# A mixture-of-experts router: gate products with the token columns stationary, choice of experts on the logits

## What is computed

```python
raw_gate = softmax(einsum('btd,de->bte', x, gate), axis=-1)      # 4096 tokens, 256 -> 16 logits
_, topk_idx = lax.top_k(raw_gate, 3)
mask = one_hot(topk_idx, 16).sum(axis=2)
gate_topk = mask * raw_gate
gate_topk = gate_topk / maximum(sum(abs(gate_topk), axis=-1), 1e-12)
hidden = relu(einsum('btd,edh->bteh', x, W1) + b1)
expert_out = einsum('bteh,ehd->bted', hidden, W2) + b2
out = einsum('bte,bted->btd', gate_topk, expert_out)
```

## Time and profile before

| | us |
|---|---|
| median of 3 runs (1891.88 to 1895.51) | 1894.03 |
| the profiled execution, its own time | 1896.07 |
| span of the profiled execution | 1894.1 |
| PE busy in the span | 1727.0 (91%) |
| DVE busy | 1362.5 (72%) |
| POOL busy | 1263.0 (67%) |
| ACT busy | 743.8 (39%) |
| routing phase (first transposes to last decoding) | 1308.4 to 1407.5 |

### The profile page before, as it was taken

How to read it: one execution, slowest core, us unless ns; L and a number is a source line. 1 busy time by engine, 2 the same in 40 slices (tenths; PEclk the granted TensorE clock), 3 DMA queues, 4 the chain that set the end, 5 groups by cost and what they waited for, 6 DMA issues and landing times. The chain is left out here.

```text
span 1894.1 us, 33741 instructions
## 1 busy us (share of the span) xinstructions
PE 1727.0 (91%) x9587; PEld 1288.4 (68%) x9588; DVE 1362.5 (72%) x3170; ACT 743.8 (39%) x1583; POOL 1263.0 (67%) x1086
## 2 busy tenths in 40 slices
PE   5389999999999999999999999998679999999970
PEld 4356766766666676667667666754349999999960
DVE  3358888888888888888888888865974544444435
ACT  3124445444445544444444445534442222222213
POOL 2138778767887786787778688833347777777753
PEclk8579999999999999999999999999659999999995
DMA  9856656755665676556657646613944444444447
GB/s 308 283 167 172 174 148 187 211 146 156 187 166 153 197 201 177 168 153 191 180 181 213 164 144 169 177 47 118 374 137 69 71 72 74 73 71 73 72 83 234
DMA packets 184483, 300.41 MB, mean 159 GB/s; under 512 B 22544, under 2 KB 81936, under 8 KB 184352
## 3 DMA queue, kind: packets, MB, share of 16 engines
q1 hardware_dynamic: 160784, 267.23, 47.8%
q0 software_dynamic: 21504, 30.29, 9.9%
q10 hardware_dynamic: 2064, 1.31, 0.2%
HBM read 186.84 MB, written 111.67 MB: 158 GB/s over the span
## 5 line engine op out<-in xcount | busy, mean ns | idle before, releaser
L735 ACT ACTIVATE prob<-b_ps 128x512 f32<-128x512 f32 (+3 forms) x768 | 354.6, 488 | 364.3 <-PE b_ps L572 260.7
L499 POOL TENSOR_TENSOR acc<-acc,prob 128x1024 f32<-128x1024 f32 (+1 forms) x192 | 353.1, 1839 | 6.4 <-POOL acc L499 3.2
L571 PE MATMUL b_ps<-q,k 128*128 128x512 f32 (+3 forms) x768 | 296.9, 391 | 9.7 <-DMA q<-mrow 5.2
L472 POOL TENSOR_TENSOR roped<-rot 128x512 f32<-128x512 f32 x128 | 175.0, 1367 | 184.6 <-DVE rot L858 183.8
L564 PE MATMUL a_ps<-k,q 128*128 128x512 f32 (+3 forms) x768 | 267.5, 385 | 18.6 <-DMA k<-scratch_hilo 9.7
L840 DVE CUSTOM_DVE_ANT_0 masked<-a_ps,causal 128x128 bf16<-128x128 f32 (+3 forms) x512 | 237.3, 479 | 58.8 <-PE a_ps L564 50.9
L653 PE MATMUL y_ps<-prob,v_sb 128*64 128x512 f32 (+3 forms) x1536 | 275.6, 494 | 0.0
L1573 DVE TENSOR_SCALAR hT<-h_ps,b1T 128x128 f32<-128x128 f32 x448 | 126.1, 344 | 197.4 <-PE h_ps L1489 158.4
L572 PE MATMUL b_ps<-q,k 65*128 65x512 f32 (+3 forms) x768 | 265.1, 349 | 0.0
L1463 POOL DMA_INDIRECT scratch_sum<-y,dst_i x112 | 177.8, 1587 | 95.6 <-ACT y L1538 90.8
L888 DVE RECIPROCAL inv<-inv 128x128 f32<-128x128 f32 x256 | 232.3, 929 | 8.6 <-ACT inv L776 6.2
(11 more groups left out here) (258 smaller groups left out, 2478.4 us busy)
## 6 DMA issues: line engine op xcount, KB each, us to landing
q<-scratch_hilo SPq DMA_DIRECT2D x192, 256.0 KB, 4.6
k<-scratch_hilo SPq DMA_DIRECT2D x192, 256.0 KB, 5.2
scratch_hilo<-hi SPq DMA_DIRECT2D x64, 512.0 KB, 4.2
scratch_hilo<-lo SPq DMA_DIRECT2D x64, 512.0 KB, 4.6
w_sb<-scratch_wsplit SPq DMA_DIRECT2D x32, 512.0 KB, 3.7
w<-in_L_ffn_W_dram SPq DMA_DIRECT2D x32, 512.0 KB, 9.3
wv_sb<-scratch_wsplit SPq DMA_DIRECT2D x16, 512.0 KB, 6.5
xT<-scratch_xsplit SPq DMA_DIRECT2D x6, 1024.0 KB, 6.9
```

Of the source, the lines that this page charges most:

```text
L499: nc.gpsimd.tensor_tensor(sums, old, probs(q), ALU.add).then_inc(m["sum_p"], 1)
L571: nc.tensor.matmul(out, k1[s][:, h, js], q1[s][:, h, qs], start=True, stop=False, skip_group_check=True)
L735: nc.scalar.activation(probs(q)[:, h, :], b_ps[:, h, 0:w], ACT.Exp).then_inc(exp_done[h], 1)
```

## The change

`gate_logits` swaps the operands: the 128 columns of a tile are stationary and the gate's half (16 columns) moves, so the logits come out with tokens on partitions, directly in the group's bank. `take_logits` (ACT) and `turn_logits` (PE) are gone, with their buffers. `choose` works on the logits in PSUM: eight largest, difference to the first of them, indices, one-hot matrices, mask; it no longer waits for the exponentials. `weigh` waits for them, multiplies them by the mask and divides by the sum of what is left. The floor of 1e-12 is gone (the largest exponential is 1).

```diff
             def gate_logits(u):
                 pe.wait_ge(m["r_xtt"], u + 1)
-                if u >= 4 and u % 2 == 0:
-                    pe.wait_ge(m["r_lt"], u // 2 - 1)
+                if u >= 8 and u % 4 == 0:
+                    pe.wait_ge(m["r_sub"], u // 4 - 1)
                 x_cols = xtt[:, u % 2, :].rearrange("p (i k c) -> p i k c", i=2, k=DK)
-                for k in range(DK):
-                    ins = nc.tensor.matmul(lt_ps[u // 2 % 2][0:E_, (u % 2) * 256:(u % 2) * 256 + 256], gate[:, k, :],
-                                           x_cols[:, :, k, :], start=(k == 0), stop=(k == DK - 1),
-                                           skip_group_check=True)
+                for i in range(2):
+                    for k in range(DK):
+                        ins = nc.tensor.matmul(logits_of(u // 4)[:, 2 * (u % 4) + i, :], x_cols[:, i, k, :], gate[:, k, :],
+                                               start=(k == 0), stop=(k == DK - 1), skip_group_check=True)
                 ins.then_inc(m["r_lg"], 1)
-            def turn_logits(v):
...
-                if u >= 3 and u % 2 == 1:
-                    turn_logits(u // 2 - 1)
...
-            turn_logits(UNITS // 2 - 1)
...
-            def take_logits(v):
...
-                if u >= 2 and u % 2 == 0:
-                    take_logits(u // 2 - 1)
...
-            take_logits(TILES // 4 - 1)
             exponents(GROUPS - 1)
...
-                dve.wait_ge(m["r_lgt"], 2 * (g + 1))
-                lg, some, sums = logits_of(g), red[:, 0, ts], red[:, 1, ts]
-                link(V.tensor_reduce(some, lg, AX_X, ALU.max))
-                V.tensor_tensor(tmp[:, ts], lg, bc(some, E_), ALU.subtract).then_inc(m["r_sub"], 1)
-                dve.wait_ge(m["r_exp"], g + 1)
-                link(V.tensor_reduce(some, prob[:, ts], AX_X, ALU.add))
-                link(V.reciprocal(sums, some))
-                link(V.tensor_tensor(prob[:, ts], prob[:, ts], bc(sums, E_), ALU.mult))
-                for t in range(ts.start, ts.stop):
-                    ins = V.max(top[:, t, :], prob[:, t, :])
+                dve.wait_ge(m["r_lg"], 4 * (g + 1))
+                lg = logits_of(g)
+                for i, t in enumerate(range(ts.start, ts.stop)):
+                    ins = V.max(top[:, t, :], lg[:, i, :])
                 link(ins)
-                for t in range(ts.start, ts.stop):
-                    ins = V.max_index(topi[:, t, :], top[:, t, :], prob[:, t, :])
-                link(ins)
-                V.tensor_reduce(some, top[:, ts, 0:TOPK], AX_X, ALU.add)
+                V.tensor_tensor(tmp[:, ts], lg, top[:, ts, 0:1].broadcast_to([P, LG, E_]), ALU.subtract)
+                for i, t in enumerate(range(ts.start, ts.stop)):
+                    ins = V.max_index(topi[:, t, :], top[:, t, :], lg[:, i, :])
+                ins.then_inc(m["r_sub"], 1)
+                dve.wait_ge(m["r_sub"], g + 1)
...
-                link(V.tensor_scalar(some, some, 1e-12, None, ALU.max))
-                V.reciprocal(sums, some)
...
-            def weigh(ts):
-                n = ts.stop - ts.start
+            def weigh(g):
+                ts = tiles_of(g)
+                some, sums = red[:, 0, ts], red[:, 1, ts]
+                dve.wait_ge(m["r_mask"], g + 1)
+                dve.wait_ge(m["r_exp"], g + 1)
                 link(V.tensor_tensor(tmp[:, ts], prob[:, ts], maskb[:, ts], ALU.mult))
-                link(V.tensor_tensor(tmp[:, ts], tmp[:, ts], bc(red[:, 1, ts], E_), ALU.mult))
+                link(V.tensor_reduce(some, tmp[:, ts], AX_X, ALU.add))
+                link(V.reciprocal(sums, some))
+                link(V.tensor_tensor(tmp[:, ts], tmp[:, ts], bc(sums, E_), ALU.mult))
```

More of the change, by code:

```diff
@@ L989, in routing_phase @@
         all_ps = ctx.enter_context(nc.psum_tensor("all_ps", [P, 512], F32))
-        lt_ps = [all_ps, pre_ps]
-        lt_sb = [slots, inc]
         bb_ps = ctx.enter_context(nc.psum_tensor("bb_ps", [P, 512], F32))
@@ L1004, in routing_phase @@
         names = ("r_slots r_begun r_ef r_row r_tile r_part r_code r_bb_sb r_inv r_stored r_bb r_bbadd r_w r_small r_const r_chain "
-                 "r_x1 r_xtr r_xtt r_lg r_lt r_lgt r_b1 r_rs r_sub "
+                 "r_x1 r_xtr r_xtt r_lg r_b1 r_rs r_sub "
                  "r_exp r_mask r_pre r_g32 r_gtr r_gt r_b2 r_b2hi r_b2lo r_zero r_gst").split()
@@ L1328, in _ @@
                 if g < GROUPS - 1:
-                    dve.wait_ge(m["r_mask"], g + 1)
-                    weigh(tiles_of(g))
+                    weigh(g)
                 if g == 2:
@@ L1335, in gate_weights @@
             def gate_weights():
-                dve.wait_ge(m["r_mask"], GROUPS)
-                weigh(tiles_of(GROUPS - 1))
+                weigh(GROUPS - 1)
                 link(V.tensor_copy(g32[:, :, 0:E_], tmp[:]))
```

## The result

| | before | after |
|---|---|---|
| median of 12 runs | 1894.55 us | 1898.55 us (1896.40 to 1905.85) |
| ratio of the runs, 95% interval | | 1.0025 (1.0015 to 1.0035) |
| span of the profiled execution | 1894.1 us | 1900.6 us |
| first transposes of the routing phase to its last decoding | 99.2 us | 106.0 us |
| last mask, counted from the first transposes | 37.6 us | 44.2 us |

The change makes the kernel slower by 4 us. The forecast was faster by 7; the first rival came. What stands outside the routing phase did not change, but the start of the phase varies: the code of the attention phase is the same in all kernels here, and the first transposes behind it started between 1300.8 and 1312.2 us.

The account below looks back on a forecast made before the run. The prediction took PE as the bound until the first group's logits, then DVE for four groups. Last mask 7.1 us earlier, weights 0.3 us longer: -6.8 us, giving a median of 1887.2 us, range 1884 to 1903.5.

Parts of the forecast that it names:

- the first rival: PE's clock falls to 1.2 GHz in the routing units, making the kernel slower: 1904.5 us, chance 0.27.
- The likeliest case: The forecast with its faster neighbour: routing phase shortened by 6.8 us, median 1887.2 us, chance 0.57.
- Part 2: PE's units: PE's routing units: removed turns save 2.4 us, swapped products add 1.2 us, last products end at 1334.9.
- the clock falls in the units: PE drops to 1.2 GHz after four routing units, adding 17.3 us to the units: 1904.5 us, chance 0.27.
- The term "products": PE's swapped gate products in each unit: 1.05 us in place of 0.97.
- The spacing: Swapped product records on PE follow each other at 0.114 us, eight of them making 0.91 us.
- the first load: First stationary load of each unit's products on PE, taken as uncovered: 0.08 us more per unit.
- Part 1: DVE's choice: 3.87 us a group up to the mask, weights 1.22 us, reads of PSUM costing no more.
- Part 3: Where PE and DVE meet: PE delivers a group every 6.6 us, DVE needs 5.1; last mask 7.1 us earlier.
- Part 4: Behind the last mask: DVE's weights add 0.3 us; waits for exponentials and the gate store cost nothing there.

Follow-up runs that it names:

- e2: Changed kernel with the choice and weights of the kernel before, so only the products are swapped and the turns gone; 1905.12 us, ratio 1.0045.
- e11: The kernel of e5 unchanged, profiled once more; routing phase 99.1 us, no median.
- e12: The kernel before, unchanged, profiled once more; routing phase 100.4 us, no median.
- e1: Kernel before with only the new order of choice and weights on DVE, old products and turns kept; 1892.38 us, ratio 0.9986.
- e9: Changed kernel, unchanged, profiled a second time; routing phase 106.1 us, no median.
- e10: Changed kernel, unchanged, profiled a third time; routing phase 106.1 us, no median.
- e5: Changed kernel plus extra 256-column float32 matmuls in units 0 to 4 and ahead of unit 4's wait for rows; 1893.61 us, ratio 0.9993 to before.
- e7: As e5, plus an extra matmul of 128 moving columns in each later unit; 1889.02 us, ratio 0.9963 to the kernel before.
- e6: Changed kernel plus an extra 256-column float32 matmul behind the transposes of every unit; 1893.23 us, ratio 0.9980 to the kernel before.
- e8: Kernel before with the new choice, and swapped products in the last four units only; 1893.26 us, ratio 0.9976.

## Why the prediction was wrong

- **The likeliest case, the step that failed.** "Part 2: PE's units" priced every unit at the full clock. That clock was the condition, and it did not hold: a unit took 2.45 us at 1.2 GHz in place of the 1.64 (0.59 + 1.05) priced, and the last products came 39.9 us after the first transposes, where they had come at 27.7 and 26.5 was forecast. The rival "the clock falls in the units" had the mechanism, and 0.27 was too little for it. A hint stood in the text: in the batches 20.80 busy us of 22 had not brought the clock back. I read it against the appearance that PE would be busy throughout, and gave the appearance more weight. I also looked for the fall after four units; in the kernel after it came at the start of the phase, behind the barrier where PE is idle for 1.05 us in any case.
- **What the swap really took away** is the recovery first, and the holding in some executions (e2, e11). e12 and e1 show the old products with the clock falling at the same place and rising 3.4 us later; with the swapped ones it stays down up to the last products (kernel after, e9, e10), and the mean clocks of all 12 executions of the result fit that. No step of the prediction asked what would bring the clock back.
- **The rival's size.** It gave 3.1 us a unit (1.64 + 1.44) and 1904.5 us. The unit was 2.45, since its base was too high: at full clock a unit is 1.28 (e5), not 1.64. With sixteen units low in place of twelve, and that smaller unit, the mask came 6.6 us late, not 10.2.
- **The term "products", mis-sized at full clock.** From the first of them to the next transposes it is 0.81 us (e2, 1309.62 to 1310.43), not 1.05. The spacing was right: in the trace of e2 the second to the eighth record start 0.112 us apart (1309.647 to 1310.317), where 0.114 was taken. Wrong was the first load, "which nothing covers now": it began at 1309.51, under the last transposes, and the second record started 0.03 us behind the first. So seven spacings are paid and not eight and a load. The way from transposes to products is 0.48, not 0.59. At 1.2 GHz the records stand 0.213 us apart (kernel after, 1319.216 to 1319.429). The Trainium skill, "TensorE: Matmul & The Clock Gate", section "LDWEIGHTS (loading the stationary operand)", gives 0.107 us for 128 columns, near the spacing at full clock but half of that at 1.2 GHz. The rule that the prediction took from that section, that the number of rows does not count, is not borne out by the turns: their loads have 16 rows and 128 columns, and their records start 0.06 us apart (kernel before, 1317.319 to 1317.443). Its section "The mechanism" would put the 16 columns on top of that, an estimate of 0.12 us, too near to 0.112 to tell; but transposes, with 128 moving columns each, start 0.109 us apart (kernel before, 1317.749 to 1317.966), and that does not fit it.
- **Part 1 was right within 0.4 us.** The last group costs 4.28 (4.27 in e1) in place of 3.87. The difference is one instruction: L1284 took 0.69 us while POOL ran its split of the second biases (1350.80 to 1351.60), where L1316 had taken 0.24. All 11 profiles with the new choice show 0.69 or 0.70 for it in the last group, always beside that split, and 0.29 in the groups without it; no run moves the split away, so the cause is likely and not shown. The maxima took 0.75 us, as from SBUF; the reads of PSUM cost nothing that shows.
- **Part 3 came out** in its structure, that DVE waits for PE ahead of each group, but by luck: PE became slower. With the clock held (e5) a unit of 1.28 us hands over a group every 5.1 us, just what DVE needs, and DVE found the logits of the second and the last group ready. **Part 4 was right:** behind the mask the phase is longer by 0.2 us (61.8 against 61.6), forecast 0.3; neither the gate store nor the exponentials of the last group held anyone up. In the first three groups DVE did wait for the exponentials (0.83, 0.84 and 0.35 us), at no cost, since it waited for PE next.
- **The gain that was meant** shows in two profiles. With the clock held the phase is 92.2 (e5) and 92.4 us (e7), 7 us shorter, the size of the forecast -6.8. That the numbers meet is in part luck: a unit was priced 0.36 us too dear, and against that e5 and e7 carry extra matmuls, and e5 3.4 us at the low clock. No run shows the kernel after itself with the clock held.

What stays open: what exactly keeps or loses the clock in bare units (e5 and e11 are the same kernel). No run here separates the loads from the short matmuls as its cause, and none aims at how the attention phase ends, which goes with the first fall.

## What to carry to other kernels

Swapping the operands of a small product can make PE's work cheaper and its clock lower: in these profiles the clock came back only in units that had float32 matmuls of 256 moving columns (e1, e5, e6, e8, e12), and a busy PE in the profile did not show that they were gone. When a change makes PE's instructions short, look at the granted clock over several executions (the mean over the span told more about e5 than its profile), at the first microseconds behind a barrier above all, and ask what would raise it again. Undoing one half of a two-part change is cheap: the choice alone gained 0.14%, the products alone cost 0.45%.

## What was not expected of the hardware

- Eight records with a stationary operand of 128 columns and 16 moving float32 columns took 0.96 us, tail included, at 2.4 GHz, and 1.73 us at 1.2 GHz. At full clock they start 0.112 us apart, and transposes with 128 moving columns 0.109: 16 moving columns were no cheaper than 128, so the moving columns do not set the pace here, and it follows the granted clock. The turns, with loads of 16 rows by 128 columns and 16 moving ones, start 0.06 us apart. They are transposes and not products, but the columns of the load alone do not set the pace either.
- Extra work made a kernel faster: e7 issues 17 float32 matmuls more than the kernel after, and is 0.6% below it (0.9963 against 1.0025, each to the kernel before as run with it; the two did not run side by side).
